# Order of turns, lag and last store in a one-core kernel of attention and expert mixture

## What is computed

```
x = x + heads(ln(x))        # 16 causal heads of 16, q = k = v = ln(x)
x = x + mixture(ln(x))      # 8 experts of 256 -> 1024 -> 256 with GELU; the best two of a batch, chosen from its mean token
x = x + distance(ln(x))     # one head: q, k, v = ln(x) @ W + b; softmax over exp(-|q - k|^2); @ Wo + bo
x = x + mixture(ln(x))      # the same weights again
```

## Time and profile before

| | |
|---|---|
| median of 3 runs | 1744.38 us (1744.10 to 1744.78) |
| profiled execution | 1745.11 us |
| its span | 1743.4 us |
| PE busy, mean granted clock | 97% of the span, 0.997 |
| ACT, DVE, POOL busy | 55%, 58%, 17% |
| exponentials of the heads (L556) | 544, 502.0 us |

### The profile page before, as it was taken

The page is one execution under the profiler, slowest core; times in us unless marked ns, Lnnn a source line. Parts: engine busy times, 40 slices in busy tenths (PEclk is TensorE's granted clock), DMA queues, the critical chain, the costliest instruction groups (busy, mean ns, idle before and its releaser), DMA issues.

```text
span 1743.4 us, 27922 instructions
## 1 busy us (share of the span) xinstructions
PE 1683.6 (97%) x10527; PEld 1152.8 (66%) x10527; DVE 1015.4 (58%) x2116; ACT 952.8 (55%) x1260; POOL 305.0 (17%) x402
## 2 busy tenths in 40 slices
PE   6999999999999999999999999999999999999998
PEld 2222222222227888888878888889888888888886
DVE  5352233344328765865556677766897876575554
ACT  6999999999995222422235444554444432242221
POOL 2112212212200000000015335534443100000000
PEclk9999999999999999999999999999999999999999
DMA  4100100000120020000000000000000200300000
GB/s 134 25 13 14 25 19 13 20 19 15 45 71 1 1 88 10 1 0 1 0 1 1 1 1 1 1 1 1 1 1 25 73 1 12 113 10 13 13 12 24
DMA packets 33681, 35.91 MB, mean 21 GB/s; under 512 B 3255, under 2 KB 30478, under 8 KB 33550
## 3 DMA queue, kind: packets, MB, share of 16 engines
q1 hardware_dynamic: 33550, 34.14, 6.6%
HBM read 22.07 MB, written 4.19 MB: 15 GB/s over the span
## 4 chain that ended last, share of the span: by engine, by line
PE 69%; ACT 14%; issue 10%; DVE 5%; POOL 0%; DMA 0%; ACTq 0%; SPq 0%; DVEq 0%
ACT a_probs L556 14%; PE f_h L794 7%; PE f_h L796 7%; PE f_h L795 7%; PE f_ypsum L796 7%; PE f_ypsum L794 7%; PE f_ypsum L795 7%; PE d_outs L794 4%; PE d_outs L795 4%; PE d_outs L796 4%; PE d_banks L794 3%; PE d_banks L796 3%; PE d_banks L795 3%; PE a_out L662 2%; PE a_scores L691 2%
## 5 line engine op out<-in xcount | busy, mean ns | idle before, releaser
L556 ACT ACTIVATE a_probs<-a_scores 128x1024 f32<-128x1024 f32 x544 | 502.0, 1159 | 8.5 <-PE a_scores L691 7.7
L1124 ACT ACTIVATE f_gelu<-f_h,f_bcol 128x512 f32<-128x512 f32 x256 | 176.6, 690 | 468.8 <-PE f_h L796 465.6
L662 PE MATMUL a_out<-a_probs,a_values 128*32 128x512 f32 (+3 forms) x2560 | 294.3, 541 | 12.0 <-ACT a_probs L556 8.8
L1179 DVE TENSOR_SCALAR f_hh<-f_gelu,f_gates 128x512 fp32r<-128x512 f32 x256 | 124.8, 488 | 236.9 <-ACT f_gelu L1124 235.7
L1611 ACT ACTIVATE d_score<-d_dist,d_nksq 128x512 f32<-128x512 f32 x128 | 92.8, 725 | 222.2 <-DVE d_dist L1754 220.4
L1181 DVE SCALAR_TENSOR_TENSOR f_hl<-f_gelu,f_gates,f_hh 128x512 fp32r<-128x512 f32 x256 | 192.4, 752 | 9.2
L691 PE MATMUL a_scores<-a_moving,a_fixed 64*128 64x512 f16 (+3 forms) x1280 | 184.5, 352 | 13.2 <-ACT a_probs L556 4.5
L691 PEld LDWEIGHTS a_scores<-a_moving,a_fixed 64*128 64x128 f16 x1280 | 47.0, 94 | 207.0 <-ACT a_probs L556 168.3
L1648 POOL TENSOR_TENSOR distance_raw<-distance_raw,d_p 128x512 f32<-128x512 f32 x112 | 146.1, 1305 | 198.5 <-ACT d_p L1586 198.3
L570 POOL TENSOR_SCALAR_AFFINE_SELECT a_probs<-a_probs 128x256 f32<-128x256 f32 (+1 forms) x224 | 97.6, 450 | 427.6 <-ACT a_probs L556 426.5
L794 PE MATMUL f_h<-c_xhi,f_w 128*128 128x512 f32 x384 | 155.0, 404 | 0.0
(11 more groups left out here) (228 smaller groups left out, 2876.9 us busy)
## 6 DMA issues: line engine op xcount, KB each, us to landing
f_raw<-in_L_ffn_W SPq DMA_DIRECT2D x24, 512.0 KB, 7.6
a_fixed<-a_moving SPq DMA_DIRECT2D x60, 96.0 KB, 2.3
out<-x SPq DMA_DIRECT2D x8, 512.0 KB, 2.9
x<-in_L_attn_a_x SPq DMA_DIRECT2D x7, 512.0 KB, 8.2
f_raw<-in_L_ffn_W SPq DMA_DIRECT2D x12, 256.0 KB, 3.6
a_fixed<-a_moving SPq DMA_DIRECT2D x60, 32.0 KB, 2.0
f_early_raw<-in_L_ffn_W SPq DMA_DIRECT2D x4, 256.0 KB, 3.4
x<-in_L_attn_a_x SPq DMA_DIRECT2D x2, 256.0 KB, 3.0
```

The source lines that it names most:

```text
L556: act.activation(probs[:, u % UR], scores[:, 2 * (u % SR):2 * (u % SR) + 2, :], ACT.Exp, scale=HD ** -0.5)\
L662: mm = pe.matmul(spare[32 * j:32 * j + 32, i % 2, skip:skip + w], values[:, G % 2, kt + tile, j, :], probs[:, u % UR, j % 2, col:col + w], ...
L1124: act.activation(gel[:, n % HR, :], hps[:, n % 2, :], ACT.Gelu, bias=mix.bcol[:, q, FT * e + j:FT * e + j + 1])\
L1179: dve.tensor_scalar(hh[:, n % HR, :], gel[:, n % HR, :], gate, None, ALU.mult).then_inc(s_hh, 1)
```

## The change

1. **Start of the heads.** DVE's list: statistics and `rest` of tiles 0 to 3 first, then normalise, halves and copy of that chunk, then the next four tiles, and so on, four times `rest` of four tiles in place of twice of eight. The second `turn_fixed` goes to bank 4 of the scores, waits for three exponentials, and ACT copies its result, ahead of unit 5, in place of DVE. `turn(1)` and `turn_fixed(1)` both stand in step 2, ahead of its products.
2. **Turns.** `turn` takes a list of tiles; the next group's turns stand in steps 15 to 18, 20 to 22, 27 to 30 and 32 to 35, mostly a tile a step. `turn_out` stands ahead of the products of its step.
3. **From the heads to the mixture.** The last two head products are in the mixture's step 0, behind `up(0)`, and the last output's turn in its step 1. PE waits at the start for exponential 543 alone.
4. **Distance.** `LAG` is 4; the halves have rings of 4 (`HR`); the turn of chunk 2 stands behind the projections of chunk 1; `add_result` is a step later, values(15) too.
5. **End.** Of the last chunk's result, the first 128 features get their bias by DVE once their matmuls are done, the others by ACT; the two turns use two banks; the store is two DMAs of two tiles (256 KB).

```diff
@@ head_attention
-        TURN_AT = {15: 0, 19: 1, 27: 2, 31: 3}
+        TURN_AT = {15: (0, (0,)), 16: (0, (1,)), 17: (0, (2,)), 18: (0, (3,)), 20: (1, (0, 1)), 21: (1, (2,)), 22: (1, (3,)),
+                   27: (2, (0,)), 28: (2, (1,)), 29: (2, (2,)), 30: (2, (3,)), 32: (3, (0,)), 33: (3, (1,)), 34: (3, (2,)), 35: (3, (3,))}
+        fixed_turned = spare[:, 1, :], scores[:, 4, :]
@@ vector
             statistics(0)
-            statistics(1)
-            first_norm.rest(dve, 0, 2 * TPC)
+            first_norm.rest(dve, 0, TPC)
             normalise(0)
             halves(0)
             low_fixed(0)
+            statistics(1, early)
+            place(0)
+            statistics(1, late)
+            first_norm.rest(dve, TPC, 2 * TPC)
             normalise(1)
-            place(0)
             halves(1)
             low_fixed(1)
-            statistics(2, early)
+            statistics(2)
             place(1)
-            statistics(2, late)
-            dve.wait_ge(s_tfix, 2)
-            dve.tensor_copy(fixed[0][:, :, CHUNK:2 * CHUNK], as_pairs(spare[:, 1, :])).then_inc(s_pfix, 1)
-            statistics(3)
-            first_norm.rest(dve, 2 * TPC, TILES)
+            first_norm.rest(dve, 2 * TPC, 3 * TPC)
             copy_out(0)
             split(2)
-            normalise(3)
+            statistics(3, early)
             place(2)
-            halves(3)
+            statistics(3, late)
+            first_norm.rest(dve, 3 * TPC, TILES)
+            split(3)
             place(3)
             finish_out(0)
@@ scalar
+                if u == 3:
+                    high_fixed(1)
+                if u == 5:
+                    place_fixed(1)
@@ tensor
-                if n == 0:
+                if n == 2:
                     turn(1)
-                if n == 1:
                     turn_fixed(1)
+                if turned_outputs < len(outputs) and n == (output_end[turned_outputs] + LAG + 1 if turned_outputs else FIRST_OUT_AT):
+                    turn_out(turned_outputs)
+                    turned_outputs += 1
                 if n >= LAG:
-                    products(n - LAG)
+                    if steps[n - LAG][2] in ("full", "first") and steps[n - LAG][3] == 0:
+                        spare_free()
+                    products(pe, n - LAG)
                 if G == 0 and n in FIRST_TURN_AT:
                     pe.wait_ge(s_ocopy, 1)
                     turn(FIRST_TURN_AT[n])
-                if turned_outputs < len(outputs) and n == (output_end[turned_outputs] + LAG + 1 if turned_outputs else FIRST_OUT_AT):
-                    turn_out(turned_outputs)
-                    turned_outputs += 1
-            for n in range(len(steps) - LAG, len(steps)):
-                products(n)
@@ mixture
+            banks_read(pe)
             for n in range(len(steps) + LAG):
                 if n < len(steps):
                     up(n)
-                if n == 0:
-                    finish_ahead(pe)
+                if n < 2:
+                    finish_ahead(pe, n)
...
             if last_layer:
-                for half in range(2):
-                    turn_result(pe, NB * CHUNKS - 1, half)
+                pe.wait_ge(s_y, KD * LAST + 1)
+                pe.wait_ge(s_y_scalar, 1)
+                for half, bank in enumerate((misc, side)):
+                    if half == 0:
+                        pe.wait_ge(s_added, (TPC // 2) * LAST)
+                    else:
+                        side_free(s_added, (TPC // 2) * (LAST + 1))
+                    turn_tokens(pe, half, bank)
...
+                for chunk in range(LAST):
+                    store(chunk * TPC, TPC)
+                for half in range(2):
+                    store(LAST * TPC + 2 * half, 2)
@@ distance_attention
-    LAG = 3
+    LAG = 4
-        QR, DR, R = 3, 2, 3
+        QR, DR, R, HR = 3, 2, 3, 4
-        phi = sb("d_phi", [P, R, CHUNK], F32R)
-        plo = sb("d_plo", [P, R, CHUNK], F32R)
+        phi = sb("d_phi", [P, HR, CHUNK], F32R)
+        plo = sb("d_plo", [P, HR, CHUNK], F32R)
-            turn(2)
             project(1, 0)
             project(1, 1)
+            turn(2)
             free_ahead(pe)
             lengths(0)
-                if 1 <= chunk < NG and at in (3, 4):
-                    add_result(chunk - 1, at - 3)
+                if 1 <= chunk < NG and at in (4, 5):
+                    add_result(chunk - 1, at - 4)
```

More of the change, by code:

```diff
@@ L369, in twice_of, with products @@
             return v.unsqueeze(2).to_broadcast([P, TPC * GH, 2, HD])
+        fixed_turned = spare[:, 1, :], scores[:, 4, :]
         def as_pairs(bank):
             return bank.bitcast(F16).rearrange("p (r n) -> p r n", r=GH // 2)
+        def products(pe, n):
+            G, c, kind, kt = steps[n]
+            i = CHUNKS * G + c
+            pe.wait_ge(s_exp, first_unit[n + 1])
+            pe.wait_ge(s_mask, masks_by[n])
+            for tile, skip, w, unit_of, col_of in pieces[kind]:
+                for j in range(GH):
+                    u, col = first_unit[n] + unit_of[j // 2], col_of[j // 2]
+                    mm = pe.matmul(spare[32 * j:32 * j + 32, i % 2, skip:skip + w], values[:, G % 2, kt + tile, j, :],
+                                   probs[:, u % UR, j % 2, col:col + w], start=(kt == 0 and kind in ("full", "first")),
+                                   stop=(kind == "last"), skip_group_check=True)
+            mm.then_inc(s_pv, 1)
         @block.sync
@@ L619, in last_group, with turn @@
                     routed.append((mix.s_bcol, 1))
[L621 to L625, removed]
+            def turn(job, tiles=range(TPC)):
+                if tiles[0] == 0:
+                    spare_free()
+                    pe.wait_ge(s_lo, job + 1)
+                for t in tiles:
                     for r in range(GH // 2):
@@ L650, in turn_out @@
                 turns[1] += 1
[L652 to L658, removed]
-                for tile, skip, w, unit_of, col_of in pieces[kind]:
-                    for j in range(GH):
-                        u, col = first_unit[n] + unit_of[j // 2], col_of[j // 2]
-                        mm = pe.matmul(spare[32 * j:32 * j + 32, i % 2, skip:skip + w], values[:, G % 2, kt + tile, j, :],
-                                       probs[:, u % UR, j % 2, col:col + w], start=(kt == 0 and kind in ("full", "first")),
-                                       stop=(kind == "last"), skip_group_check=True)
-                mm.then_inc(s_pv, 1)
             pe.wait_ge(pr.s_made, 3)
@@ L715, in _, with finish, scores_read, probs_read @@
                 if n % GS in TURN_AT and G + 1 < NG:
[L716 removed]
+                    job, tiles = TURN_AT[n % GS]
+                    turn(CHUNKS * (G + 1) + job, tiles)
                 if G == NG - 1:
                     last_group(n % GS)
[L719 to L720 removed]
             assert turned_outputs == len(outputs) - 1
[L723 to L729 removed]
+        def finish(pe, part):
+            if part == 0:
+                for n in range(len(steps) - LAG, len(steps)):
+                    products(pe, n)
+            else:
+                pe.wait_ge(s_ocopy, len(outputs))
+                for t in range(TPC):
+                    mm = pe.transpose(spare[:, 1, t * P:(t + 1) * P], osb[:, 1, t * P:(t + 1) * P], pr.ident[:])
+                mm.then_inc(s_oturn, 1)
+        def scores_read(pe):
+            pe.wait_ge(s_exp, len(units) - 1)
+        def probs_read(engine):
+            engine.wait_ge(s_pv, len(steps))
+        def output_read(engine):
             engine.wait_ge(s_added, len(outputs))
[L733 removed]
+        return finish, scores_read, probs_read, output_read
 class Columns:
@@ L998, in beside, with turn_tokens @@
             return work
+        def turn_tokens(pe, half, bank):
+            for t in range(2):
+                for k in range(KD):
+                    token = (2 * half + t) * P
+                    mm = pe.transpose(bank[:, (t * KD + k) * P:(t * KD + k + 1) * P], ysb[:, k, token:token + P], pr.ident[:])
+            mm.then_inc(s_rturned, 1)
         def turn_result(pe, chunk, half):
```

122 lines of the change are left out of this document (67 added, 55 removed).

## The result

The changed kernel takes 1740.25 us (median of 18 runs, 1737.23 to 1741.26) against 1744.49 (18 runs, 1743.04 to 1745.87): a ratio of 0.9972, interval 0.9965 to 0.9979. It is faster, by 4.2 us and not by the 12.8 of the forecast. The profiled execution took 1740.63, its span 1738.9.

A forecast was written before the change was run, and what follows sets the result against it. Outside the heads TensorE work in fixed order was taken to bound the kernel, in the heads ACT's exponentials. Start +3.2, heads -7.0, seam -1.4, distance -5.2, end -2.4 sum to -12.8: median 1731.6 us, range 1724 to 1739.

The forecast's parts named there:

- The start: Start of the heads: first exponential 3.5 us earlier, then PE waits for job 3 and loses clock; net +3.2 us.
- -0.8 net of idle time: In DVE's list up to job 3's residue: a 1.84 us wait goes, 1.0 is given back for new waits.
- third rival: At the start, added chains fit in time DVE has anyway, so the 3.5 us come in full: 1724.9, chance 0.09.
- first rival: Clock stays low longer: 1.2 us more at the start, 1.0 at the seam: 1733.8, chance 0.18.
- The groups: In the heads, quarter turns and output turns ahead of products remove three stalls of a group: -7.0 us.
- (a): In a group, step 15's turn held the next scores back 0.54 us; quarters save 3.0 over all groups.
- (b): At group boundaries, the output's turn delayed scores 0.59 us; ahead of products it saves 2.9 over five of seven.
- (c): In a group, the turn at step 19 ahead of a narrow last step: 0.2 us in each of 7, 1.4.
- its new wait: At two group boundaries, the output's turn ahead of products waits for the output's copy: 0.3 us each, +0.6.
- The seam: From heads to mixture: moved products fill PE's stand, products and turn gain 1.1 and 0.3 us from the clock: -1.4.
- Distance: Distance stage: longer lag -4.0 us, its end -2.1, its start +0.9; together -5.2.
- End: End of the kernel: conversion -0.7 us, second turn at once -1.05, smaller store -0.65; together -2.4.

The follow-up runs named there:

- merged_chain: The changed kernel with statistics of tiles 12 to 15 and one chain of eight tiles ahead of the first output's copy: 1734.03 us.
- products_first: The changed kernel with the products of step 0 ahead of turn(1) and turn_fixed(1) in step 2: 1737.41 us.
- output_turn_behind: The changed kernel with the output's turn behind the products of its step again, the quarters kept: 1742.12 us.
- copies_first: start_both with all 16 gathers behind the copy and addition of output 24, and weights' splits q and k behind those of output 28: 1730.44 us.
- start_alone: The kernel before with the new start of the heads alone: 1750.01 us.
- products_not_moved: The changed kernel with the last two head products at the end of the heads again, the last output's turn still in step 1: 1741.55 us.
- start_both: The changed kernel with one chain for tiles 8 to 15 ahead of the first output's copy and step 0's products ahead of turn(1): 1731.96 us.
- whole_turns: The changed kernel with whole turns in steps 15, 19, 27 and 31, the output's turn still ahead of the products: 1738.99 us.
- half_turns: start_both with the next group's turns in halves of two tiles, in steps 15, 16, 18, 19, 27, 28, 31 and 32: 1732.22 us.

## Why the prediction was wrong

**The start, forecast +3.2, was +7.8: this step alone holds 4.6 of the 8.3 us that are missing.** The failed step is "-0.8 net of idle time: the 1.84 goes, and I give back 1.0". I put every item of DVE's list behind the other and let the idle time be small. By the two windows under the result, DVE's work until job 3's residue grew by 4.0 us (I had 3.7), and its idle time grew by 2.2 where I had it shrink by 0.8. DVE stood 4.25 us for that copy, with a chain and the statistics of tiles 12 to 15 written behind it, and job 3's turn ran at 36.93 where I had 33.5. merged_chain shows it: the same work ahead of the copy, and 6.6 us come back. My reading against the third rival was off too: from 11.20 to 30.55 DVE is busy for 17.52 of 19.35 us, so idle for 1.8 and not 1.1. The first products, which feed the copy, were later than I thought, since they stood behind both turns, the turned chunk's copy and a stretch at half speed; products_first shows these 3.1. The low clock behind the stand, which I had put at 1.5, cost 2.6 (43.98 - 36.93 against 36.19 - 31.76). That is the 1.2 more that my first rival had for the start, without its fall at the seam. How much of it an execution pays is luck: the trace of output_turn_behind has the same stand of 3.44 us and no fall, its 19th exponential comes at 40.83, and of the 18 runs of the changed kernel the three with a mean granted clock of 1.000 took 1737.2 to 1737.8, the ten with 0.997 took 1740.2 to 1741.3.

**The groups, forecast -7.0, gave -3.3.** The failed step is the sum: I took the stalls (a), (b), (c) as separate. The move of the output's turn, which I had at -2.9 for (b) and +0.6 for its new wait, gives 3.5 by itself, since the stall at the 31st exponential, which I had given to the quarters as (a), goes with it. The quarters, at 3.0 and 1.4 for (a) and (c), then gave 0.11 a regular group and cost 0.2 over the stage. (c) never came: the 40th exponential loses at least as much as before in every kernel. That the stalls share PE's spare 0.26 us a step would explain this; it is argued and not shown. A quarter costs 0.22 and not 0.14, within my bounds, and whole and half turns give nearly the same regular group, so there it wasn't decisive. The new wait of the output's turn was right in place and too small: 0.9 and 0.6 in place of 0.3 each, which copies_first gets back.

**The seam, -2.0 for -1.4:** the size came out near, in part by luck. The trace of before has a fall of the clock there, and I took it as the rule; in the two other traces with a stand at this place it didn't fall, and against start_alone, one of these, the seam gains 0.1. Where it falls, the loss is 1.6 us up to the output's turn, of which 1.1 is in the 24 products (2.57 against 1.44), as I had it; the rest up to the turn was larger than my 0.3.

**Distance, -4.4 for -5.2.** The waits for the low half fell from 13 to 3, below the 8 that I had named, and the lengths' waits for POOL's squares took the place that I had given them, 0.95 and 1.20. The reorder, of which I expected 0.55, gave nothing. Against the 128th gelu, the 112th score of the stage comes 4.2 us earlier, the 128th 4.9, and the part behind it takes 0.5 more, so of the 2.1 that I booked to the end only 0.7 came there, and was mostly lost again. The waits don't explain the whole gain: PE's idle time in the stage fell by 1.7 (7.6 to 5.9), its busy time, which has modelled ends, by 2.6. That this is the restarts, as I had it, no run shows.

**End, -2.6 for -2.4:** as worked out, the two turns follow each other. From the modelled end of the last value matmul, as my 9.6 and 7.3 were counted, it takes 7.0.

Of the rivals, "the start isn't late" was the furthest off. None had the start as the one bad part, and my bound of +5 for it was too narrow: it allowed for idle time not regained, not for work locked behind a wait.

## What to carry over

When work is split into smaller pieces, look at what in the list stands between the pieces: work written behind an item that waits is late by the whole wait, however small it is. Savings of stalls close to each other need not add; cost the second with the first one gone. And PE may go on at half speed after an idle stretch, so a stall there can cost more than its length; how much more differs from execution to execution, so compare runs whose granted clocks agree.

## What the runs showed of the chip

- Idle stretches of PE of like length were followed by the low clock in one execution and not in another: 1.75 us with a fall to 0.50, 1.45 without one at the same place in start_alone and products_not_moved, 2.04 with one in start_both's trace, and there four other executions whose times and clocks speak against one. The clearest case is the stand of 3.44 us for job 3, which three kernels have with the same instructions in front of it. The rows are from output_turn_behind and then whole_turns, in each the turn and a window behind it, columns as in the earlier trace rows; those of the changed kernel stand under the result:

```profile
36.41 0.61 PE L651 MATMUL a_out<-ident,a_split_m 128*128 128x128 f16 x8 [3.44 <-DVE a_split_m L445]
38.00:40.00 2.00, 2.00 (x22) 0.47 (x15) 0.00 (x0) 2.00 (x3) 1.38 (x4) 1.00 0.29 65
...
37.35 1.01 PE L650 MATMUL a_out<-ident,a_split_m 128*128 128x128 f16 x8 [3.44 <-DVE a_split_m L444]
40.00:42.00 2.00, 2.00 (x20) 0.69 (x16) 0.25 (x1) 1.72 (x2) 1.53 (x4) 0.93 0.44 99
```

  The first had no fall, the second a short one, the changed kernel one that lasted until 42.9; the 19th exponential came at 40.83, 43.07 and 43.98. The Trainium skill, "TensorE: Matmul & The Clock Gate", Part 1, says that the gate's watch on activity runs freely and isn't started by the kernel, so where a transition falls differs from run to run. These rows agree with that; they don't prove it. What the Trainium skill says of transposes on that page, in Part 4, which stands beside my first rival, no run separated; but whole_turns and the changed kernel have the same two turns behind the stand (job 3's and the first output's), and the low stretch ended earlier in one than in the other.
- The granted clock in the profile's windows reads 1.00 in all windows from 13 to 27 us, also where products take 1.86 us instead of 1.00.
- Two fp16 transposes of 128x128 between other instructions hold PE for 0.22 us (146.30 to 146.52 above), four for 0.33 (109.08 to 109.41 in half_turns), eight for 0.54: by these three a piece costs some 0.1 beside 0.055 a transpose, an estimate.
